# Two bf16 pieces made on ScalarE and VectorE in place of GpSimd, and attention's sums one unit later

## The reference

```python
# L0 attention, causal, 16 heads of 16, with a rotary part of 32 shared by the heads
c_kv = x @ W_kv_down
k_rope = rotary(c_kv @ W_k_rope); q_rope = rotary(x @ W_q_rope)
k, v, q = c_kv @ W_k_up, c_kv @ W_v_up, x @ W_q
scores = (q . k + q_rope . k_rope) / sqrt(16 + 32), masked
attn = softmax(scores) @ v; return attn @ W_o
# L0 ffn: ternary weights and a fast-weight product
h = bitlinear(x, w_fc) + gate * (x @ v.T @ fast_b.T @ u.T); return bitlinear(relu(h) ** 2, w_proj)
# L1 mixer: cumulative sums of p_w*cos(k*theta) and p_w*sin(k*theta) over time, divided by the sum of p_w,
#           times a query, silu, @ W_out
# L1 ffn: relu(x @ W1 + b1) @ W2 + b2
```

## Time and profile before

| | us |
|---|---|
| median of 3 runs | 1418.54 |
| lowest and highest run | 1416.97, 1419.03 |
| the profiled execution | 1416.25 |
| its span, first to last instruction | 1414.4 |
| mean granted clock of PE, share of full | 0.933 |

### The profile page before, as it was taken

How to read it: one execution, slowest core, us unless ns; L and a number is a source line. 1 busy time by engine, 2 the same in 40 slices (tenths; PEclk the granted TensorE clock), 3 DMA queues, 4 the chain that set the end, 5 groups by cost and what they waited for, 6 DMA issues and landing times.

```text
span 1414.4 us, 22664 instructions
## 1 busy us (share of the span) xinstructions
PE 1228.1 (87%) x7820; PEld 777.4 (55%) x7820; DVE 1090.1 (77%) x2259; ACT 1047.3 (74%) x2101; POOL 333.9 (24%) x317
## 2 busy tenths in 40 slices
PE   5988987997899998999899998999999988977447
PEld 2564664464546655556556764665655655533224
DVE  3683258979878998889878998899888988586930
ACT  4674589687986889588978889597959897448522
POOL 3942202320122300430133101320133001300101
PEclk9798997899999999999999999999999999977759
DMA  8401414232215121521415131521242040022100
GB/s 264 84 22 26 102 31 129 74 83 56 83 37 138 42 83 55 121 52 24 137 44 129 23 100 45 135 47 50 94 94 64 24 137 23 23 77 67 38 0 15
DMA packets 72018, 101.49 MB, mean 72 GB/s; under 512 B 10640, under 2 KB 44064, under 8 KB 71904
## 3 DMA queue, kind: packets, MB, share of 16 engines
q1 hardware_dynamic: 71904, 100.03, 27.1%
HBM read 74.31 MB, written 25.69 MB: 71 GB/s over the span
## 4 chain that ended last, share of the span: by engine, by line
PE 55%; DVE 18%; ACT 14%; issue 7%; DMA 2%; SPq 2%; POOL 1%; POOLq 0%; DVEq 0%; ACTq 0%
PE ps L866 19%; PE ps L876 15%; DVE work L1488 6%; PE ps L949 5%; PE ps L931 5%; DVE work L1411 4%; PE ps L923 4%; PE ps L1017 3%; ACT work L1184 3%; ACT work L1177 2%; ACT xnd L1120 2%; DVE work L1497 1%; SPq L622 1%; PE ps L858 1%; DVE work L1479 1%
## 5 line engine op out<-in xcount | busy, mean ns | idle before, releaser
L1488 DVE TENSOR_TENSOR_SCAN work<-work 128x512 f32<-128x512 f32 x256 | 309.2, 1241 | 42.7 <-ACT work L1244 40.7
L1177 ACT ACTIVATE work<-work 128x384 f32<-128x384 f32 (+3 forms) x512 | 264.4, 558 | 69.7 <-DVE work L1411 68.9
L1411 DVE CUSTOM_DVE_ANT_0 work<-ps,work 128x384 f32<-128x384 f32 (+3 forms) x512 | 227.9, 486 | 92.1 <-PE ps L923 89.3
L747 POOL TENSOR_TENSOR later_norms<-later_norms,singles 128x2 f32<-128x2 f32 x112 | 103.3, 923 | 731.7 <-ACT xnd L1120 408.9
L931 PE MATMUL ps<-ident,work 128*128 128x128 f32 x1280 | 202.7, 284 | 16.8 <-ACT work L1184 9.0
L931 PEld LDWEIGHTS ps<-ident,work 128*128 128x128 f32 x1280 | 152.3, 145 | 87.2 <-issue 44.8
L1184 ACT COPY work<-ps 128x512 f32<-128x512 f32 x300 | 170.8, 573 | 5.6 <-PE ps L931 5.4
L1497 DVE TENSOR_TENSOR work<-work 128x1024 f32<-128x1024 f32 x128 | 158.7, 1240 | 5.3 <-DVE x L1333 0.2
L923 PE MATMUL ps<-work 96*128 96x384 bf16 (+3 forms) x512 | 123.6, 308 | 9.2 <-ACT work L1184 4.5
L866 PE MATMUL ps<-led_xTd,wf 128*128 128x512 f32 x256 | 120.2, 623 | 4.2 <-issue 4.2
L866 PE MATMUL ps<-led_xTd,wfc 128*128 128x512 f32 x256 | 118.4, 595 | 1.0 <-ACT led_xTd L1104 0.8
(11 more groups left out here) (174 smaller groups left out, 1932.0 us busy)
## 6 DMA issues: line engine op xcount, KB each, us to landing
work<-values SPq DMA_DIRECT2D x64, 256.0 KB, 3.2
work<-ratios SPq DMA_DIRECT2D x64, 256.0 KB, 4.2
scratch<-work SPq DMA_DIRECT2D x32, 384.0 KB, 4.8
work<-scratch SPq DMA_DIRECT2D x64, 192.0 KB, 3.8
work<-scratch SPq DMA_DIRECT2D x64, 128.0 KB, 4.0
x_in<-x SPq DMA_DIRECT2D x8, 512.0 KB, 6.5
work<-scratch SPq DMA_DIRECT2D x64, 64.0 KB, 4.1
values<-work SPq DMA_DIRECT2D x16, 256.0 KB, 3.0
```

Source lines behind the costliest of these rows:

```text
L1177: i = s_.activation(part_of, part_of, ACT.Exp, scale=-1.0, bias=nmax[:, row:row + 1])
L1411: i = v_.tensor_tensor_reduce(sc[:, n % 4, at:at + nk], out_of(b, name)[:, at:at + nk], base_of(qt), -SCORE_SCALE, BIG, ALU.add, ALU.min, ...
L1488: v_.tensor_tensor_scan(ring[:, at, m, :], pwr[:, slot, :], ring[:, at, m, :], 0.0, ALU.mult, ALU.add).then_inc(*scanned.one)
```

## The change

- `LAG_PV` and `LAG_OT` grow by one: PV and OT come one step later in the list of attention's items, and the list has one more step.
- POOL's items `q` and `k` go. New items: `qmid` and `kmid`, on ACT, cast a half of `rest` to the second piece. `qlow` and `klow`, on DVE, subtract it from `rest` for the third piece. Each signals and waits by half.
- `MERGE` is new for all engines, so items of all chains stand in other places.
- `work` has 32 more words, which nothing uses.

```diff
-LAG_T, LAG_PV, LAG_OT = 3, 4, 15
+LAG_T, LAG_PV, LAG_OT = 3, 5, 16
...
-    items = ["ckv", ("q", 0), ("q", 1), ("pieces", 0), "qr", ("k", 0), ("k", 1), ("pieces", 1), "kr", ("v", 0), ("v", 1),
+    items = ["ckv", ("q", 0), ("q", 1), ("qmid", 0), ("qmid", 1), ("qlow", 0), ("qlow", 1), ("pieces", 0), "qr", ("k", 0), ("k", 1), ("kmid", 0), ("kmid", 1), ("klow", 0), ("klow", 1), ("pieces", 1), "kr", ("v", 0), ("v", 1),
...
-    for n in range(ALL + 6):
+    for n in range(ALL + 7):
...
     "dve":
-        "a9 p8 a24 p a4 p a9 p a8 p9 a4 p a9 p a8 p a4 p a14 p2 a2 m a34 d a6 d a21 d a4 d a3 d a4 d a4 d a2 "
...
+        "a9 p8 a6 p a6 p2 a16 p9 a23 p a8 p2 a7 p2 a14 p a11 m a35 d a4 d a25 d a4 d a7 d a4 d a2 d a4 d m2 d "
...
-        words = 28832
+        words = 28864
...
-                if item in ("q", "k"):
-                    pieces, pick = (q_pieces, (1, 2)) if item == "q" else (k_pieces, (1, 0))
-                    is_drained(pool, b, f"{item}{n}")
-                    pool.sem_inc(waits_taken, 1)
-                    g_.tensor_copy(pieces[:, n, pick[0], :], rest[:, n, :]).then_inc(*second_piece.one)
-                    need_given(pool, second_piece)
-                    g_.tensor_tensor(pieces[:, n, pick[1], :], rest[:, n, :], pieces[:, n, pick[0], :],
-                                     ALU.subtract).then_inc(*third_piece.one)
...
+                if item in ("qmid", "kmid"):
+                    kind, pieces = item[0], (q_pieces if item == "qmid" else k_pieces)
+                    is_drained(act, b, f"{kind}{n}")
+                    s_.copy(pieces[:, n, 1, :], rest[:, n, :]).then_inc(*second_piece.one)
...
+                if item in ("qlow", "klow"):
+                    pieces, third, at = (q_pieces, 2, n + 1) if item == "qlow" else (k_pieces, 0, DC + n + 1)
+                    need(dve, second_piece, b, at)
+                    v_.tensor_tensor(pieces[:, n, third, :], rest[:, n, :], pieces[:, n, 1, :], ALU.subtract
+                                     ).then_inc(*third_piece.one)
```

More of the change, by code:

```diff
@@ L158 @@
     "pe": "xT ckv q qr k kr v base S T PV OT attnT out fxT fc fproj zxT z total query gather oout gxT gc gproj prep",
-    "act": "ystats fstats fystats zstats oystats gstats gystats centre norm xT q k v S T PV attnT fnorm fxT fc znorm zxT z weights query turn fold cos sin silu gnorm gxT gc gsum ternary prep",
+    "act": "ystats fstats fystats zstats oystats gstats gystats centre norm xT q k v S T PV attnT fnorm fxT fc znorm zxT z weights query turn fold cos sin silu gnorm gxT gc gsum ternary prep qmid kmid",
     "dve": "stats ckv q qr k kr base S T OT sum fsum z weights ratio total rates turn frac scan mix gate silu "
-           "osum gystats ternary prep tables means late",
-    "pool": "stats q k ystats fstats fc fystats zstats oystats gstats gystats gsum ternary tables late",
+           "osum gystats ternary prep tables means late qlow klow",
+    "pool": "stats ystats fstats fc fystats zstats oystats gstats gystats gsum ternary tables late",
     "sp": "fetch pieces group z kv ratio rates pw inv gsum",
@@ L168 @@
     "pe":
[11 rows of a table removed]
-    "act":
[16 rows of a table removed]
-    "dve":
[12 rows of a table removed]
[11 rows of a table added]
+    "act":
[16 rows of a table added]
+    "dve":
[14 rows of a table added]
     "pool":
[2 rows of a table removed]
+        "a p9 a3 d17 a3 d18 a3 d18 a d4 a2 d18 a3 d22 a d4 a2 d18 a3 d26 a2 d34",
     "sp":
[3 rows of a table removed]
+        "d a14 d m d m2 d m6 d2 m8 a7 d3 m5 d m8 a3 m a2 m d m2 d2 a2 d2 m3 d m4 d m6 a5 m4 a d3 a d2 m6 d m2 "
+        "d m5 a5 m4 d a d2 a d m4 d2 m4 d m5 a5 m4 a d3 a d2 m5 d m4 d m4 a5 m4 d a d2 a d m d m d m6 d m9 d4 "
+        "m4 d2 m8 d m5 d4",
 }
```

## The result

The changed kernel takes 1432.4 us, median of four runs (1429.2 to 1439.0), against 1417.8 us for the kernel before (four runs as well, 1415.9 to 1419.0). The ratio is 1.011, with a 95% interval of 1.0094 to 1.0127. So the change costs 14.7 us by the medians (13 to 18 by the interval), where the forecast was 6.5. The profiled execution took 1434.0 us.

A forecast was written before the change was run, and what follows sets the result against it. PE was taken as the bound, DVE close behind. Start 12.9 - 2.5, later sums -3 - 2, pieces +3 - 2 gave +6.4 on 1416.25 us: 1422.7, plus 2.3 to the runs' median, forecast 1425 us, range 1405 to 1440.

The forecast's parts named there:

- The start, 12.9 less 2.5: Program start: DVE waits for POOL's subtraction before unit 0, +12.9 us; half the sums' waits there return, -2.5; net 10.4.
- the sign named for a right forecast: After batch 0's attention, which ends about 10 us later, the span to the end is about 4 us shorter.
- the 10 named as a sign of error: PE's idle time in the five middle batches moving by more than 10 us either way would show the forecast wrong.
- The pieces, "I take half, +3 us": Head of a batch: casts on ACT and subtractions on DVE cost 6.5 us by chain shares, half covered by dense matmuls.
- The pieces earlier, -2: Last k piece leaves a few us earlier on two engines, saving PE's 2.1 us wait for loads: -2 us, or nothing.
- The later sums, -3 and -2: Longer lag cuts attention sums' waits for ACT's copies: -3 us from 107 to 424 us, -2 from 424 to 1160.
- my first rival: All listed waits of sums, S and loads go, 26.5 us, against start 10.4 and load 3: 1405 us, chance 0.25.
- The third rival: Later sums gain nothing, as ACT's copies come at the same distance wherever PE lacks work: +11.4, 1430 us, chance 0.10.
- The subtraction at 1.52 us: Each new DVE subtraction could take 1.52 us through contention with GpSimd, making the sum +11; not taken, 0.684 kept.
- DVE as the bound: Rival: DVE becomes the bound and the new work counts in full, +25 us, 1444 us, chance 0.15.

The follow-up runs named there:

- b_start: Kernel before, with the changed kernel's place for the start's fast-weight preparation steps on DVE and PE; 1429.6 us, ratio 1.0088.
- b_act_end: Kernel before, with only ACT's last exp and copies of batch 1's attention moved behind the mixer's cosines and sines; 1428.7 us, ratio 1.0080.

## Why the prediction was right and wrong

**Direction and range were right, the size was not**: 14.7 us and not 6.5. Two steps failed. The pieces' work was taken as half covered, and the doubling shows 65 to 72% of such work paid. The longer lag was taken as a gain of 5 us and ACT's new order as free; the trace shows the waits moved to T and S and grown by 14.4 us, and one passage of ACT's new order costs 10.5 us in the old kernel. The start, priced too high for the new order, hid part of both.

- **The start, 12.9 less 2.5.** The delay was right to 0.4 us: unit 0 at 59.60 where 59.24 was worked out, with POOL's subtraction as what ends DVE's idle time. The price is right in the old order (b_start, 11.4 us against 10.4). In the changed kernel it is smaller: 5.8 us are missing at the end of batch 0's attention, 3.9 in the time. From there to the end the span did not become 4 us shorter, the sign named for a right forecast, but 12 longer. PE's idle time in the middle batches moved by 9.8 us, just under the 10 named as a sign of error.
- **The pieces, "I take half, +3 us": the first step that failed.** Durations were right: subtractions 0.684 us as taken, casts 0.620 for 0.584. The cover was wrong. I said that long blocks of dense matmuls stand over the head of a batch. In the old order the pieces cost 13.2 us, four times that, and doubling them adds 27 to 30 in either order. The trace of before had a hint that I passed over: PE's products at the head already waited for the rotary part (1.0 and 1.1 us), so DVE was at times no further on than PE there, and work ahead of the rotary part could be paid. The chain's share (18% of the span) is an average over stages and says nothing of one stage.
- **The pieces earlier, -2.** PE's wait for the stacked pieces is 3.3 us and not less.
- **The later sums, -3 and -2, and ACT's order at nothing: the second step that failed.** The sums' waits fell by 25.6 us and not by 5. That they would go was my first rival, and it was right of the sums and wrong of the time: T and S took over all of it and 14.4 us more. The third rival comes near in its number (1430), but not in its reason: the sums don't wait any more, others wait in their place. The prediction asked only what the lag does to the instruction that waits, not which bank the next ones take. And it gave ACT's queue no price, where b_act_end measures 10.5 us. The lag alone has no price either: 112 us slower in the old table.
- **The subtraction at 1.52 us.** By the Trainium skill, SBUF — State Buffer, "Who interferes with whom", a DVE instruction with two SBUF inputs contends with a GpSimd instruction that reads SBUF. The trace of before agrees: the addition of the earlier trace rows took 1524 ns at 732.6 us, where POOL's subtraction ran beside it for 1.0 us. With POOL's pieces gone the same line, 1342 in the changed kernel, is even:

```profile
L1342 DVE TENSOR_TENSOR work<-work x16: 680/680/867, 25.9 to 1069.4; 32x512 f32<-32x512 f32 x16
```

The new subtractions stay between 665 and 695 ns. Only 3 of the 32 have any instruction of POOL beside them, so the 0.684 of the sum held because POOL had left, as the prediction said.

- **DVE as the bound.** It gave the full load as 1444 us. The doubling shows 65 to 72% paid, so that rival was nearer to the mechanism than the forecast was.

Added up from single edits in the old order: 11.4 (start) + 13.2 (pieces) + 10.5 (ACT's passage in batch 1) = 35.1 us. The change has 14.7. So the rest of the new order with its lag gives back some 20 us, if the parts add. They need not: in the new tables the start is worth 3.9, and the pieces taken back make it 13.5 us slower. How the 14.7 divide inside the changed kernel stays open beyond that; what was put back there one by one (passage, pieces, lag) made it slower.

## What to carry to other kernels

Where a queue's order is written out, one edit of a lag or of an engine can't be priced by waits that it removes: find which bank or buffer the following instructions take, and which long block stands ahead of the copy that frees it. Look at what stands behind work that moves to another engine: here an instruction behind it freed the bank that PE wanted next. Waits of 1 us on that engine in the trace of before were the hint, and doing the work twice measured how much is paid. A price holds for its order alone: the same exchange cost 13.2 us in one and gained 13.5 in the other. A stall at the start in the wrong place is easy to foresee, but its price depends on what else that order can fill it with.

## What was not expected of the hardware

Nothing contradicts the rows of before, but some prices are worth having. A load of the activation table took 1.28 us on ACT. One stands ahead of the mixer's cosines at 241.78 us and one ahead of the exp behind them at 253.03, so one passage of cosines between two exp costs two of them. The new cast from SBUF to bf16 took 620 ns where the one from PSUM takes 584. The subtraction takes 684 ns on DVE and 1216 on POOL, so that POOL's four pairs, 7.9 us a batch, became 5.2 us on two engines, and in the old order the kernel became slower.
